# A new order of the work on every engine of a two-layer transformer, Mamba and mixture-of-experts kernel

## The reference

```python
xn = layernorm(x)
x = x + L0_attn(xn) + L0_ffn(xn)
xn = layernorm(x)
x = x + L1_attn(xn) + L1_ffn(xn)

# L0_attn ("A"): 16 heads of 8, softmax(q k^T) + a position table, Wo, layer norm, W1, W2, layer norm
# L0_ffn  ("B"): six nodes, one behind the other, each an attention with 8 heads of 16
for c in range(6):
    q, k, v = ew[c, 0] * (nodes[c-1] @ We[eq]), ew[c, 1] * (nodes[a] @ We[ek]), ew[c, 2] * (nodes[m] @ We[ev])
    nodes[c] = act_w[c] * mha(q, k, v, Wq[c], Wk[c], Wv[c], Wo[c]) + q
# L1_attn: a Mamba block (in-projection, convolution, 16 states scanned over 256 positions), then a GELU FFN
# L1_ffn : router over 8 experts, top 2, each expert silu(xn @ W1[e]) @ W2[e]
```

## Time and profile before

| | |
|---|---|
| median of 3 runs | 1455.35 us (1451.99 to 1456.02) |
| profiled execution | 1454.89 us, span of its instructions 1453.1 us |
| PE busy | 1192.4 us, 82% |
| DVE busy | 990.3 us, 68% |
| ACT busy | 735.7 us, 51% |
| POOL busy | 256.2 us, 18% |
| mean granted TensorE clock | 0.928 of 2.4 GHz |

### The profile page before, as it was taken

The page is one execution under the profiler, slowest core; times in us unless marked ns, Lnnn a source line. Parts: engine busy times, 40 slices in busy tenths (PEclk is TensorE's granted clock), DMA queues, the critical chain, the costliest instruction groups (busy, mean ns, idle before and its releaser), DMA issues.

```text
span 1453.1 us, 27405 instructions
## 1 busy us (share of the span) xinstructions
PE 1192.4 (82%) x10600; PEld 834.4 (57%) x10600; DVE 990.3 (68%) x1549; ACT 735.7 (51%) x1277; POOL 256.2 (18%) x262
## 2 busy tenths in 40 slices
PE   6667787768996899869997899879996899678768
PEld 5435454445774567546774577546764577346527
DVE  2323335786769776896768776886779776976785
ACT  1224344745456555745564555646465555544513
POOL 1000002122112311231102311231113210231100
PEclk9879898979999999989997999979999999889979
DMA  7280020002111211102110111102110211001202
GB/s 222 45 88 1 2 52 5 31 16 49 35 48 34 57 27 63 34 16 52 60 49 19 45 23 63 34 16 53 60 49 16 49 34 45 19 31 51 77 1 77
DMA packets 117519, 63.48 MB, mean 44 GB/s; under 512 B 79440, under 2 KB 99440, under 8 KB 117392
## 3 DMA queue, kind: packets, MB, share of 16 engines
q1 hardware_dynamic: 115664, 57.89, 16.0%
q10 hardware_dynamic: 1728, 3.83, 0.8%
HBM read 54.35 MB, written 6.83 MB: 42 GB/s over the span
## 4 chain that ended last, share of the span: by engine, by line
PE 58%; ACT 16%; DVE 15%; issue 8%; DMA 2%; ACTq 0%; POOL 0%; DVEq 0%; POOLq 0%; SPq 0%
PE strips L807 9%; PE strips L792 9%; ACT probs L1095 8%; PE ps L996 8%; PE ps L984 6%; PE attn_out L820 6%; DVE rowmax_B L1321 4%; DVE hb L1450 4%; PE ps L740 3%; DVE rowmax_A L1321 3%; ACT da L1175 2%; PE ps L838 2%; DVE hb L1445 2%; PE attn_out L827 2%; PE ps L749 2%
## 5 line engine op out<-in xcount | busy, mean ns | idle before, releaser
L1095 ACT ACTIVATE probs<-strips 128x2048 f32<-128x2048 f32 x128 | 240.3, 1877 | 95.4 <-PE strips L807 95.0
L1321 DVE TENSOR_REDUCE rowmax_B<-strips 128x8 f32<-128x2048 f32 x96 | 219.8, 2290 | 92.9 <-PE strips L792 92.5
L807 PE MATMUL strips<-qs_b,ks_b 32*128 32x256 f32 x1536 | 117.3, 421 | 48.1 <-ACT probs L1095 37.2
L792 PE MATMUL strips<-ks_b,qs_b 32*128 32x256 f32 x1536 | 125.3, 445 | 35.8 <-ACT probs L1095 15.9
L1450 DVE TENSOR_TENSOR_SCAN hb<-da,hb 128x1024 f32<-128x1024 f32 x64 | 150.9, 2358 | 4.2 <-ACT da L1175 2.2
L1551 DVE SCALAR_TENSOR_TENSOR work<-eh_t,ps 128x512 f32<-128x512 f32 x128 | 85.8, 685 | 72.3 <-ACT eh_t L1222 71.4
L996 PE MATMUL ps<-ze,w_e 128*128 128x256 f32 x512 | 129.0, 390 | 6.9 <-DVE ctx_b L1333 2.8
L984 PEld LDWEIGHTS ps<-w_e,work 128*128 128x128 f32 x1024 | 122.7, 192 | 5.8 <-issue 2.9
L984 PE MATMUL ps<-w_e,work 128*128 128x128 f32 x1024 | 125.3, 276 | 0.4 <-DVE acc L1534 0.4
L1175 ACT ACTIVATE da<-dt,a_neg 128x255 f32<-128x255 f32 x256 | 108.5, 498 | 17.1 <-DVE hb L1450 16.8
L807 PEld LDWEIGHTS strips<-qs_b,ks_b 32*128 32x128 f32 x1536 | 75.9, 196 | 70.4 <-issue 54.0
(11 more groups left out here) (236 smaller groups left out, 1899.8 us busy)
## 6 DMA issues: line engine op xcount, KB each, us to landing
w_e<-in_w_e SPq DMA_DIRECT2D x128, 256.0 KB, 3.1
qs_a<-a_scr SPq DMA_DIRECT2D x8, 512.0 KB, 3.8
ks_a<-a_scr SPq DMA_DIRECT2D x8, 512.0 KB, 4.9
pos<-t_scr SPq DMA_DIRECT2D x8, 384.0 KB, 15.9
a_scr<-qkv_a SPq DMA_DIRECT2D x16, 128.0 KB, 3.7
qs_b<-maxrow SPq DMA_DIRECT2D x96, 4.0 KB
x_in<-in_x SPq DMA_DIRECT2D x8, 128.0 KB, 3.1
a_scr<-ks_a SPq DMA_DIRECT2D x2, 512.0 KB, 7.3
```

Source lines behind the costliest of these rows:

```text
L792: mm = pe.matmul(o, strip(qs, b, kind, g, j, qc * P, P), strip(ks, b, kind, g, j, 0, L), start=True, stop=True)
L807: mm = pe.matmul(o, strip(ks, b, kind, g, j, kc * P, P), strip(qs, b, kind, g, j, 0, L), start=True, stop=True)
L1095: act.activation(probs[:, group % 2, :, :, :].rearrange("p h a b -> p (h a b)"), strips[:, :], ACT.Exp).then_inc(s_exp, 1)
L1321: dve.tensor_reduce(out=rowmax[kind][:, b % sides_n, k % 2, :, :], in_=strips[:, :].rearrange("p (h q t) -> p h q t", h=4, q=2), axis=AX, ...
```

## The change

No instruction, buffer, wait rule or stage is added or removed. All but one of the 48 numbers of `START`, and nearly all of `PLACES`, are new, on all five engines. The number of rows of TensorE's program is the same before and after (1313). Since banks are taken in turn in TensorE's order, the banks and the uses that are waited for change with it.

```diff
 START = {
-    "cell": [83, 24286, 48519, 72773, 96992, 121248, 145454, 169691],
+    "cell": [110, 24434, 48646, 72859, 97105, 121332, 145553, 169814],
...
-    "one": [34, 24253, 48447, 72723, 96956, 121178, 145329, 168739],
-    "two": [0, 24235, 48451, 72714, 96923, 121156, 145650, 165592],
+    "one": [17, 24184, 48360, 72643, 96876, 121103, 145299, 168121],
+    "two": [0, 24210, 48472, 72691, 96915, 121182, 145370, 164444],
 }
```

More of the change, by code:

```diff
@@ L156 @@
+        "one": [124230, 124954, 125963, 126907, 128204, 128285, 128834, 129451, 130507, 130536, 131619, 131764, 132559, 133026, 133902, 133906,
+            136433, 136789, 137449, 138822, 139388, 139405, 140056, 140527, 141004],
+        "two": [140181, 142257, 142705, 142725, 143651, 144104, 144109, 144643, 145931, 145977, 147497, 147504, 147752, 147761, 148080, 148360,
+            149290, 150138, 150139, 150199, 151251, 151256, 152049, 152061, 152574, 154204, 154315],
     },
     "gpsimd": {
[L158 removed]
```

74 lines of the change are left out of this document (35 added, 39 removed), and 8 rows, old and new, of the table PLACES.

## The result

The changed kernel takes 1464.24 us, the median of 20 executions (1447.6 to 1469.89); the kernel before took 1454.8 us in 20 executions taken beside it (1450.89 to 1459.64). The ratio is 1.0054, with a 95% interval from 1.004 to 1.0069: 0.54% slower. Forecast were 1445 us and a gain. The profiled execution took 1460.41 us, with a span of 1458.6 and a granted clock of 0.920 (before: 0.928).

The account below looks back on a forecast made before the run. A chain over PE, ACT and DVE bounds the state stretch; PE is full in the expert stretches. Six passes 6.0, start 0.9 and end 3.4 sum to 10.3 us: median 1445, forecast range 1438 to 1451.

Parts of the forecast that it names:

- Term 1: State stretch: nt of node 3 comes earlier on ACT, so k, q, fill and reduction follow; gain 0.8 us a pass.
- slower, by place 1 alone: State stretch: ctx 3 behind late values of A delays nt each pass; above 1459.7, at 1463 us, chance 0.13.
- I cost that move at nothing; the cover is DVE's chain: State stretch: moving a state stage ahead of the next transposes only shifts TensorE's stall while DVE is busy; cost nothing.
- Term 2: DVE behind state 7: post_b 4 and post_a 2 swapped, so the next reduction starts later; loss 0.3 us a pass.
- Term 3: Scores 10 and 11: router and one transpose move into PE's waits there; gain 0.6 us a pass.
- is fixed by ACT and DVE: Chain from the fill at 834.54 over two scores and exponentials to the fill at 844.80 keeps its length.
- the later of the two copies ends at the same time: Swapping k and q leaves the first fill of the two-score chain at 834.5.
- Term 4: Expert stretches: other small moves, q of nodes 2 and 3 closer behind its node; loss 0.1 us a pass.
- Term 5: Start: q of sequence 1 moves into the 1.78 us stall before the score of group 5; gain 0.9 us.
- Terms 6 and 7: Last pass and end: score 10 and expert work fill waits, experts move ahead of L952, less rank's delay; together 3.4 us.
- The clock: Clock kept up: below 1438, at 1436 us, chance 0.15; clock falling in every pass: 3 us more each, chance 0.03.
- no-change rival: State stretch gains absorbed by DVE's work, end gains halved; 1451 to 1459.7 us, chance 0.22.

Follow-up runs that it names:

- place 1 alone: Kernel before with ctx 3 behind the values of A on TensorE and nt ahead of out_sb on ScalarE, from the third sequence on: 1452.0 us, ratio 0.9987.
- Part c: Kernel before with state 4 behind max A2 and rows B8, v 4 later, ScalarE's da of state 5 ahead of rows B8: 1460.9 us, ratio 1.0034.
- part d alone: Kernel before with post_b 4 ahead of post_a 2 on VectorE, and rows B9 and rows B1 moved: 1458.6 us, ratio 1.0028.
- end_new: Kernel before with the new order only from q of node 0 of the last sequence on: 1458.8 us, ratio 1.004.
- the tail alone: Kernel before with the new order only behind node 5 of the last sequence: 1457.6 us, ratio 1.0014.
- expert_new: Kernel before with the new order only outside the state stretch of five passes, SyncE and GpSimd included: 1463.9 us, ratio 1.0067.

## Why the prediction was wrong, by its own steps

**Term 1 (place 1, 0.8 a pass): the chain was right, the pass was not like the others.** In the pass that was worked out, place 1 alone has `nt` 1.6 us earlier, counted from score 0 of A (776.14 less 744.07, against 776.44 less 742.73; forecast 1.4), and the fill 0.6 earlier at full clock. The step that failed is "The passes are alike ... so I work out one pass and take it six times": they are alike in busy time, but in the list of TensorE only this one had `node` 3 ahead of the `values` of A. Since the numbers of `START` lie only nearly evenly, neighbours in the sorted list can change places from pass to pass. In sequences 2 and 5, where `nt` stood 31.94 us behind score 0 of A, place 1 moves it back by 0.1, so the rival's mechanism came true there in the small. The second step that failed is "that idle time is all that there is to gain: I take 1.1 of it if the fill runs at full clock": at full clock there was none, and the reduction gained 0.17 us. And "it starts as before since it waits for an exponential" failed in the changed kernel, where the swap makes that fill 0.6 us later. What is left of term 1 is 0.1 us in six passes; whether the 3 us of the median are more than the clock's spread is not shown.

**The move that was not costed: 8 us.** The prediction listed the ScalarE order of place 1 from the `exp` of group 1 of A on. The piece 10 us ahead of it, two neighbours swapped, had no term, so it stood in the sum at nothing. By the runs it is the largest single cost that was found (8.3 us added alone, 10.6 taken out), and it is why a forecast of faster became slower. The rival "slower, by place 1 alone" named 1463 us, near the 1464 that were measured, but its cause is not the one that acted; that it lies near is luck.

**"I cost that move at nothing; the cover is DVE's chain": wrong beside the old place 1, not shown beside the new.** Part c cost 5.8 us alone; the waits of 3.25 and 1.19 us are new, but whether they lengthen the chain by themselves was not separated from the clock (0.9 us at the same clock).

**Term 2 (0.3 a pass): right in size for part d alone, by luck.** The forecast was about 2 us and the run gave 3.5 in the median and 1.5 at the same clock. But that comes from `post_b` waiting for PE, 1.3 us in the pass shown; the swap on DVE that was costed costs 0.0 there in the changed kernel.

**Term 3 (place 2, 0.6 a pass): failed** in "is fixed by ACT and DVE" and in "the later of the two copies ends at the same time": ACT's own order had changed inside the chain, which takes 10.83 us instead of 10.26; the first fill waits 0.27 us for `qs_b`, score 10 waits 0.46, `wo_y` 0.44. The wait before `score` 11 fell from 1.60 to 1.25, not to 0.4. **Term 4** can't be told apart.

**Term 5 (start, 0.9): not seen**, 0.9998 (0.9975 to 1.0021); a gain of 0.9 lies within that.

**Terms 6 and 7 (3.4): not seen.** The shift ahead of L952 was right, but the end costs with end_new 4 us, which contains two of the seven swaps ahead of exp 6, and the tail alone gains nothing.

**The clock: too small a chance.** It stood with 0.03 for the loss. The changed kernel ran at a median clock of 0.915 against 0.927, and at equal clock both take 1456.5 us. By the slope of 0.78 us for 0.001 that is 9.4 us, all of the difference. This does not make the clock a cause of its own: undoing one swap on ACT brought the time back, and with it the median clock from 0.915 to 0.922. Which of the two comes first in an execution was not tested by forcing the clock.

The sum of what was forecast was 10.3 us faster. In its place stand 8 us for the swap, next to nothing for terms 1 to 3 and nothing to be seen for terms 5 to 7, and what the parts do to each other, which is of the same size: those that were run alone add up to some 16 us slower by the median, and the whole change to 9. The other pieces of the expert stretches, which make expert_new 8.8 us slower, are an open end. One sum is off in the no-change rival: without term 1 a pass keeps 0.2, so six passes give 1.2 and not "3 x 0.6", and the case 3.8 us instead of 4.4; its range would hardly move.
